# Attention, projection and routing of a decoder layer as one program, with P made transposed by a second score product

## What is computed

```python
x = x + mixer(layernorm(x), ...)
# attention, Q from layernorm(x), K and V from the context (8, 256, 256)
q = Q @ WQ + bQ;  k = K @ WK + bK;  v = V @ WV + bV          # split into 16 heads of 16
scores = einsum('bhqd,bhkd->bhqk', q, k) / 4
scores = where(causal, scores, -inf)
probs = softmax(scores, axis=-1)
x = x + einsum('bhqk,bhkd->bhqd', probs, v).reshape(B, L, 256) @ WO + bO
# experts, on layernorm(x): y is its input
logits = y @ router_w.T                                      # 2048 tokens, 8 experts
k_probs, k_idx = top_k(softmax(logits), 2);  k_probs = k_probs / sum(k_probs)
# rank of each pair within its expert by order of tokens, kept below a capacity of 641
h = silu(buf[e] @ w1[e]);  out_buf[e] = h @ w2[e]
x = x + y + sum over the 2 experts of k_probs * out_buf[expert, slot]
```

## Time and profile before

| | |
|---|---|
| median of 3 runs | 873.04 us (870.11 to 873.97) |
| the profiled execution | 866.73 us |
| its span, first to last instruction | 864.9 us |
| PE, PEld busy | 684.1 us (79%), 597.3 us (69%) |
| DVE, ACT, POOL busy | 599.8 us (69%), 434.1 us (50%), 349.4 us (40%) |
| granted TensorE clock, mean | 0.894 |
| DMA | 70.35 MB, mean 81 GB/s |

### The profile page before, as it was taken

The page is one execution under the profiler, slowest core; times in us unless marked ns, Lnnn a source line. Parts: engine busy times, 40 slices in busy tenths (PEclk is TensorE's granted clock), DMA queues, the critical chain, the costliest instruction groups (busy, mean ns, idle before and its releaser), DMA issues. The chain is left out here.

```text
span 864.9 us, 15113 instructions
## 1 busy us (share of the span) xinstructions
PE 684.1 (79%) x4776; PEld 597.3 (69%) x4792; DVE 599.8 (69%) x1285; ACT 434.1 (50%) x971; POOL 349.4 (40%) x322
## 2 busy tenths in 40 slices
PE   3759979889752199888988666509999999999992
PEld 2538768777542066666666556508999999999992
DVE  6685786867841089999999686704877877877831
ACT  4555736535411077777777311104655655655641
POOL 1357352343403000000000437752477777777755
PEclk9898999999975599999999765557999999999997
DMA  9102018230211611111111423223055255251213
GB/s 299 29 26 88 24 50 291 71 117 20 88 49 49 204 37 49 47 45 44 49 48 26 140 80 104 78 67 132 5 143 148 30 145 147 30 146 18 27 22 41
DMA packets 54857, 70.35 MB, mean 81 GB/s; under 512 B 10843, under 2 KB 45542, under 8 KB 54800
## 3 DMA queue, kind: packets, MB, share of 16 engines
q1 hardware_dynamic: 45584, 61.82, 22.1%
q0 software_dynamic: 9216, 7.81, 6.3%
HBM read 42.57 MB, written 28.79 MB: 83 GB/s over the span
## 5 line engine op out<-in xcount | busy, mean ns | idle before, releaser
L1114 ACT ACTIVATE a_pr<-a_scores,a_nm 128x128 f32<-128x128 f32 (+1 forms) x256 | 90.6, 426 | 80.8 <-DVE a_nm L1186 77.6
L1694 DVE SCALAR_TENSOR_TENSOR w_v<-w_th,w_bank 128x324 f32<-128x324 f32 x128 | 62.9, 492 | 70.6 <-ACT w_th L1424 69.3
L1563 PE MATMUL w_bank<-w_w2h,w_hh 128*108 128x256 f32 x384 | 108.6, 283 | 0.5 <-POOL w_hl L1349 0.5
L1563 PE MATMUL w_bank<-w_w2h,w_hl 128*108 128x256 f32 x384 | 107.8, 281 | 0.0
L1563 PE MATMUL w_bank<-w_w2l,w_hh 128*108 128x256 f32 x384 | 107.5, 280 | 0.0
L1424 ACT ACTIVATE w_th<-w_bank 128x324 f32<-128x324 f32 x128 | 56.6, 442 | 100.0 <-PE w_bank L102 99.9
L1349 POOL TENSOR_TENSOR w_hl<-w_v,w_hh 128x324 fp32r<-128x324 f32 x64 | 56.4, 882 | 91.5 <-ACT w_hh L1430 91.5
L1183 DVE TENSOR_REDUCE a_mx<-a_scores 128x2 f32<-128x512 f32 (+1 forms) x96 | 65.4, 681 | 34.1 <-remote 33.5
L1365 POOL IOTA w_x<- 128x16 uint32 x1 | 0.2, 191 | 205.9 <-POOLq L1077 205.9
L102 PE MATMUL w_bank<-w_xh,w_w1h 128*128 128x324 f32 x256 | 81.1, 317 | 1.1 <-ACT w_xh L1419 1.1
L102 PE MATMUL w_bank<-w_xh,w_w1l 128*128 128x324 f32 x256 | 80.8, 316 | 0.0
(11 more groups left out here) (230 smaller groups left out, 1995.6 us busy)
## 6 DMA issues: line engine op xcount, KB each, us to landing
w_s<-in_L_ffn_w SPq DMA_DIRECT2D x16, 1024.0 KB, 5.9
disp<-c_blank SPq DMA_DIRECT2D x8, 658.1 KB
w_rows<-disp SPq DMA_DIRECT2D x8, 658.1 KB
vd<-m_vs SPq DMA_DIRECT2D x4, 816.0 KB, 3.7
a_vs<-vd SPq DMA_DIRECT2D x1, 3264.0 KB, 11.1
g_x<-in_x SPq DMA_DIRECT2D x4, 512.0 KB, 7.9
m_cin<-in_ctx SPq DMA_DIRECT2D x4, 512.0 KB, 4.3
kd<-m_qkh SPq DMA_DIRECT2D x4, 512.0 KB, 2.9
```

Source lines behind the costliest of these rows:

```text
L1114: ins = act.activation(pr[:, u % 2, j * n:(j + 1) * n], sbank[u % 3][:, j * n:(j + 1) * n], ACT.Exp, bias=nm[:, u, j:j + 1], scale=SCALE)
L1563: mm = pe.matmul(eb[t // 2][0:SP_, (t % 2) * D:(t % 2 + 1) * D], a[:, g % 3, s], w2_piece(b, f), start=f == 0 and t % 2 == 0 and n == 0, s ...
L1694: dve.scalar_tensor_tensor(v[:, n % 4, :], th[:, n % 2, :], 1.0, hb[n % 3][:, 0:HALF], ALU.add, ALU.mult).then_inc(F["v"], 1)
```

## The change

The mixer stays, but for V: DVE writes V with its bias once, in fp32, into `vf`, where each head has 32 columns, 16 of V and 16 of zeros (`VP`); the splitting on ACT and POOL goes, and `vd` is 2048 x 512 fp32. WO is no longer loaded or split there.

Attention, projection and routing become one block, `attention_route_experts`, of which one step serves a third of a batch and half. There are 16 groups g (8 batches b, 2 halves k of the heads) of 3 steps, so 48 steps. In a group there are 8 heads, as 4 pairs p and 2 row halves e (partitions 0 to 63 and 64 to 127). Rows 0 to 15, 16 to 31 and 32 to 47 of each half hold Q high, high, low and K high, low, high, so that one matmul with 48 rows makes the split product.

- Scores are made twice. Once as queries by keys, six steps ahead (LEAD), for the maxima alone: `mask(u)`, `scores(u)`, and one reduction of 1024 columns on DVE (`maxima(u)`). Then as keys by queries (`turned_mask`, `turned`), where K has two more rows of -1 and Q two more rows that hold the maxima, high and low, so that the product comes out with the maximum subtracted.
- To get there the maxima of a group are turned by PE (`turn_maxima`), split by ACT and DVE, and written into Q's rows by 16 DMAs of one row each (`maxima(g)` on SP).
- ACT takes one exponential of 1024 columns per step, from PSUM to SBUF in fp32. This is P transposed; no transpose and no split follows.
- The product with V has V stationary (32 columns) and P moving, in fp32, the four heads of a set in four groups of 32 output rows; the same again with ones gives the sums (`weigh`). DVE takes a reciprocal of 128 x 256 and multiplies (`divide`), which leaves the output transposed, as the projection needs it.
- Projection (fp32, WO not split) and routing of each block are spread over later steps: `batch_due` and `due` say that batch b is projected at step 8 + 6b, and that block i of 512 tokens has its layer norm at 12i + 16, its logits at 12i + 20, its ranks at 12i + 23, and its 8 scatters at steps 12i + 24 to 12i + 31. The layer norm's scaling moves from DVE to ACT.
- SP lays each group's Q and K by 12 DMAs of 64 KB (16 rows x 4 pairs x 256). Four groups have room (ITEMS); group g + 2 is laid ahead of the maxima of group g.
- The scores and the turned scores have one pair of PSUM banks each, so that a step of PE waits for DVE's reduction and ACT's exponential of the step before.

The diff, cut to its core:

```diff
-                def lay(b, k):
-                    ge(sp, S[f"s{k}"], UPC * b)
-                    for src, q, kx in ((0, qh, kxh), (1, ql, kxl)):
-                        sp.dma_start(q[:, k, :].bitcast(F32), qd[src][k * P:(k + 1) * P, bass.ds(b * L, L)]).then_inc(S[f"laid{k}"], 16)
-                        for h in range(HPC):
-                            rows = slice(h * HD, (h + 1) * HD)
-                            sp.dma_start(kx[rows, k, h, :].bitcast(F32), kd[src][k * P + h * HD:k * P + (h + 1) * HD, bass.ds(b * L, L)])\
-                                .then_inc(S[f"laid{k}"], 16)
...
+                def lay(g):
+                    b, k = divmod(g, 2)
+                    ge(sp, A["st"], 3 * (g - ITEMS + 1))
+                    for m, srcs in ((q3[g % ITEMS], (qd[0], qd[0], qd[1])), (k3[g % ITEMS], (kd[0], kd[1], kd[0]))):
+                        for n, src in enumerate(srcs):
+                            heads = src[k * P:(k + 1) * P, b * L:(b + 1) * L].rearrange("(p e r) t -> e r p t", p=4, e=2)
+                            for e in range(2):
+                                at = 64 * e + HD * n
+                                sp.dma_start(m[at:at + HD, :, :].bitcast(F32), heads[e]).then_inc(A[f"laid{g % ITEMS}"], 16)
+                def maxima(g):
+                    sp.wait_ge(A["ml"], g + 1)
+                    for n in range(2):
+                        for e in range(2):
+                            for p in range(4):
+                                at, h = 64 * e + 3 * HD + n, 4 * e + p
+                                sp.dma_start(q3[g % ITEMS][at:at + 1, p, :].bitcast(F32), mt[g % 2][h:h + 1, n, :].bitcast(F32))\
+                                    .then_inc(A[f"m_in{g % 2}"], 16)
...
+                for g in range(GR):
+                    if ITEMS <= g + 2 < GR:
+                        lay(g + 2)
+                    maxima(g)
+                    if g == 0:
+                        weights(1)
+                    if g % 2 == 1 and 3 <= g and (g - 3) // 2 + 2 < B:
+                        values((g - 3) // 2 + 2)
+                    if g % 4 == 3 and g >= 7:
+                        store_base((g - 7) // 4)
...
+                def exps(n):
+                    act.wait_ge(A["st"], n + 1)
+                    ge(act, A["pv"], n - 2)
+                    act.activation(pr[n % 3][:, :], tbank[:, :], ACT.Exp, scale=SCALE).then_inc(A["exp"], 1)
...
+                                lhs = ones[:, h, :] if part else v32[b % 2][:, t, head * VP:(head + 1) * VP]
+                                mm = pe.matmul(obank[g % 2][32 * j:32 * j + 32, part * L + L - w:part * L + L], lhs,
+                                               pr[n % 3][:, at:at + w], start=s == 0 and part == 0, stop=True,
+                                               skip_group_check=True)
...
+                for t in range(-LEAD, END):
+                    u = t + LEAD
+                    if batch_due(t) is not None:
+                        project(batch_due(t))
+                    for j in range(2):
+                        if due(t, TURN + j) is not None:
+                            x3_turn(due(t, TURN + j), j)
+                    if due(t, LOGITS) is not None:
+                        logits(due(t, LOGITS))
+                    if due(t, RANKS) is not None:
+                        ranks(due(t, RANKS))
+                    if 0 <= t < NS:
+                        turned_mask(t)
+                    if u < NS:
+                        mask(u)
+                    if 0 <= t < NS:
+                        turned(t)
+                    if u < NS:
+                        scores(u)
+                    if t % 3 == 0 and 0 <= t // 3 + 1 < GR:
+                        turn_maxima(t // 3 + 1)
+                    if 1 <= t <= NS:
+                        weigh(t - 1)
...
+                    if u < NS:
+                        maxima(u)
+                    if t % 3 == 0 and 0 <= t // 3 + 1 < GR:
+                        maxima_low(t // 3 + 1)
+                    if t % 3 == 0 and 1 <= t // 3 <= GR:
+                        divide(t // 3 - 1)
```

More of the change, by code:

```diff
@@ L37 @@
 NEG = -1e30
-VW = HD + 1
-VT = HEADS * 3 * VW
+VP = 2 * HD
 MIX = {}
@@ L314, in _ @@
                 sp.wait_ge(S["k_st"], 32 * NBLK)
-                for n in range(2):
-                    sp.wait_ge(S[f"v_st{n}"], 16 * NBLK // 2)
+                sp.wait_ge(S["v_st"], 16 * NBLK)
                 sp.wait_ge(S["blanked"], 16 * E)
@@ new lines, in mask @@
+                def mask(u):
+                    s = u % 3
+                    ge(pe, A["nm"], u)
+                    for e in range(2):
+                        bank = sbank[:, e * 4 * P:(e + 1) * 4 * P]
+                        out = bank.rearrange("q (p k) -> q p k", p=4) if s == 0 else \
+                            bank.rearrange("q (p k) -> q p k", p=2)[:, :, P:2 * P]
+                        n = 4 if s == 0 else 2
+                        pe.matmul(out, c["identb"][:, :], c["mask"][:, :].unsqueeze(1).to_broadcast([P, n, P]),
+                                  start=True, stop=False, skip_group_check=True)
@@ new lines, in scores @@
+                def scores(u):
+                    g, s = divmod(u, 3)
+                    if s == 0:
+                        pe.wait_ge(A[f"laid{g % ITEMS}"], LAID * (g // ITEMS + 1))
+                    q, kx = q3[g % ITEMS], k3[g % ITEMS]
+                    todo = [(p, e) for p in (range(4) if s == 0 else (2 * s - 2, 2 * s - 1)) for e in range(2)]
+                    for n, (p, e) in enumerate(todo):
+                        rows, keys = slice(64 * e, 64 * e + 3 * HD), P if s == 0 else L
+                        tok = slice(0, P) if s == 0 else slice(P, L)
+                        at = e * 4 * P + (p if s == 0 else p % 2) * keys
+                        mm = pe.matmul(sbank[:, at:at + keys], q[rows, p, tok], kx[rows, p, 0:keys], start=False,
+                                       stop=True, skip_group_check=True)
+                    mm.then_inc(A["s"], 1)
@@ new lines, in turned_mask @@
+                def turned_mask(n):
+                    s = n % 3
+                    ge(pe, A["exp"], n)
+                    for e in range(2):
+                        bank = tbank[:, e * 4 * P:(e + 1) * 4 * P]
+                        out = bank.rearrange("k (p q) -> k p q", p=4) if s == 2 else \
+                            bank.rearrange("k (p q) -> k p q", p=2)[:, :, 0:P]
+                        m = 4 if s == 2 else 2
+                        pe.matmul(out, c["mask"][:, :], c["identb"][:, :].unsqueeze(1).to_broadcast([P, m, P]),
+                                  start=True, stop=False, skip_group_check=True)
@@ new lines, in project @@
+                def project(b):
+                    if b == 0:
+                        pe.wait_ge(S["rw"], 16 * 9)
+                    pe.wait_ge(A["o"], 2 * b + 2)
+                    if b % 2 == 0:
+                        ge(pe, S["xt"], b)
+                    else:
+                        pe.wait_ge(S["x2"], b)
+                    for t in range(2):
+                        for k in range(DC):
+                            at = (b % 2) * L + t * P
+                            mm = pe.matmul(bank0[:, t * D:(t + 1) * D], ot[:, k, at:at + P], wo[:, k, :],
+                                           start=k == 0, stop=k == DC - 1)
+                    mm.then_inc(S["y"], 1)
```

600 lines of the change are left out of this document (253 added, 347 removed).

## The result

| | before | after |
|---|---|---|
| median | 871.58 us (867.26 to 873.97, 4 runs) | 904.91 us (904.56 to 905.85, 4 runs) |
| profiled execution, span | 866.73, 864.9 us | 904.72, 903.0 us |
| granted TensorE clock, mean | 0.894 | 0.858 |

The change is slower: a ratio of 1.039, 95% interval 1.0345 to 1.0435. The prediction was 860 us, range 838 to 896, with 0.34 on slower: wrong in sign and outside the range.

What follows compares the result with a forecast made beforehand. SP's queue of DMA issues was to bound the groups at 13.5 us each; with start, last steps and tail the fetch came 11.7 us earlier, 12.7 with the mixer, giving 854.0 profiled, plus 6.3: 860 us, range 838 to 896.

Steps and rivals of the forecast that it cites:

- The step that failed: In SP's queue, every DMA issue was priced at about 0.473 us whatever its size, the sixteen maxima rows included.
- its 61 issues: SP's issues ahead of the first maxima, put at 28.9 us, plus 2 us for one stall.
- SP's queue: Main forecast for the groups: 28 issues at 0.473 us, 13.5 us per group with other transfers; chance 0.52.
- the cheap side: Rival on SP's issues: 0.42 us each, 12.6 us per turn of the maxima, 844 us in all; chance 0.15.
- The loop: From one group's maxima to the next: landing 2.0 us, chain of engines 3.9, sixteen issues 7.6, together 13.5 us.
- PE as the bound: Rival: matmuls in `weigh` take turns and tiling changes cost; at 16 us per group about 901 us, slower; chance 0.20.
- The clock: Rival: PE idles at landings and gets a lower clock; 15 us per group, 881 us, no gain; chance 0.13.
- The tail: Last block's chain from V's product through projection and routing to the scatters' landing: 33.2 us, after three steps of about 3 us.

Runs made afterwards that it cites:

- the kernel by way of DRAM: The changed kernel with each group's maxima written to DRAM by one DMA and brought back by two, instead of 16 one-row DMAs: 821.65 us, ratio 0.9464.
- the kernel whose waits are gone: The kernel by way of DRAM with the transposes of a normed block one step later (TURN 18 instead of 17): 806.39 us, ratio 0.9312.
- the kernel with four kinds: The changed kernel without its row DMAs, plus 16 transfers per group into an unread array, in four forms by turns: 865.8 us (before: 865.37).

## Why the prediction was wrong

**The step that failed.** "An issue costs SP this whatever it moves: 16 KB or 128 KB." The rows that stood for it differ in size and share their kind, DRAM to on-chip memory. The sixteen new issues are of another kind, on-chip to on-chip and cut in 32 packets, and cost SP 0.63 us each. Their term, 16 x 0.473 = 7.6 us per group, measured 10.2 in the mean of the twelve groups (10.0 in most). The twelve loads came out at 6.7 instead of 5.7, mostly by one issue of about 1.4 us among them (457.22 above). That issue is not the rows' doing: in the kernel by way of DRAM the loads still take 6.2 in the mean, 5.5 (2.66 + 2.77) without such an issue and up to 6.8 with one. What makes it long stays open.

Term by term, from the sum as predicted to the trace: SP's start and its 61 issues 1.9 us early; the first two groups' maxima, up to 335.0, 2.3 late in total; twelve groups with loads 206.5 us instead of 162 (17.2 each, not 13.5), which is 44.5 of the 49.9 us; the last two 28.8 instead of 27; landing 1.2 instead of 2.0; steps and tail 44.3 instead of 42.2. Of the 3.7 us per group the rows are 2.6, the loads 1.0 and the load of V and the store 0.1.

**Where the forecast was right.** SP's queue bounds, without a hole, PE waits for `a_q<-a_mt` at each group, DVE is at 43% ("under 60"). The text named as its failure "an issue of one row costs other than 0.47", but beside a doubt of 0.05 either way it worked out only the cheap side, 0.42, taken from a row of the same kind. An operation that no row showed had to be bounded from both sides, and this one was not.

**The loop.** I had it equal to the queue: 2.0 + 3.9 + 7.6 = 13.5. Measured it is 4.5 us from the last row's issue to the next group's first (540.95 to 545.43) plus 10.1, 14.6 us. The 4.5 stand where I had 2.0 + 3.9: PE starts 1.1 us after the last issue's end (542.06), and the rest is 3.4, since the chain goes there from PE's transposes of the maxima (to 544.57) straight to the two copies, without the reduction that I had put in. The rows made both longer; the queue, 17.2, is the longer one, as it also carries the loads, which no longer fit into the wait.

**PE as the bound.** The rival said slower, and slower it was, but not by this; the sign came true by another mechanism. V's product in PE's timeline after, in mid-stage:

```profile
441.44 0.64 PE L1411 MATMUL a_out<-a_pr,a_v 128*32 128x256 f32 x8
441.89 0.61 PE L1411 MATMUL a_out<-a_pr,a_ones 128*32 128x256 f32 x8
442.44 0.23 PE L1473 MATMUL a_shared<-w_both,c_onesb 128*128 128x24 bf16 x3
```

Four fp32 products of 256 columns (recorded as eight) start to start in 0.45 us. Four of the same length on all 128 columns of the array, the projection, take 1.99 at the same granted clock of 1.00, and 1.83 to the start of the next matmul (427.91):

```profile
426.08 1.99 PE L1439 MATMUL a_shared<-w_wo,a_ot 128*128 128x256 f32 x8
```

So the four column groups do run side by side: 4.1 times as fast from start to start. By FP8 and Floating Point Precision (TensorE Precision Notes) of the Trainium skill true FP32 takes four passes; 1024 columns at 0.45 ns would then be 1.84 us alone and 0.46 side by side, and the traces agree with both. The 5.5 us that I took as the least for V's product per group is 2.7 at the full clock (four sets of 256 columns at 0.45 and four of 128 at 0.22, 579.88 to 580.12). Three steps of PE in the midst of waiting took about 10.2 us (436.41 to 446.6), in the range of 10 to 12, and PE is the fullest engine once the rows are cheap, at 11.0 to 12.5 us per group, which gains and doesn't lose. What the changes between matmuls of full, half and quarter size cost was not isolated.

**The clock.** 0.78 in the groups against 0.98 in attention before. PE waited for 82 us there, as that rival said, but the clock is not the cause: the sixteen rows take SP 10.0 to 10.8 us in all twelve groups, and the clock is back at 0.96 in the kernel whose waits are gone. There it came as a second gain beside the 8.1 us of waiting.

**The tail.** It is right within 2.1 us of 42.2, with errors of both signs. The last product with V is done 9.4 us after the landing, where 9.0 and 2.0 had been put; the division, with the wait for it, took 3.8 instead of 1.1, since a reciprocal alone takes 1.76; the projection 3.44 at the lower clock, instead of 3.0. In the mixer 2.4 us went, not 1 (Q's store is issued at 266.29 instead of 268.69); the kernels here differ among themselves by up to 3.8 us at SP's first load after the mixer (276.63 to 280.38), so that is within what this part varies.

## What to carry to other kernels

A price read from rows holds for the kind in the rows: before a DMA's issue price is multiplied by hundreds, compare source and destination memory and the number of packets, not only size, and where no row matches, say what twice the price would do to the sum. If many small transfers stand in a loop in which an engine waits for them, count the issues first: here three issues through DRAM, with one more landing, beat sixteen direct ones by 81 us. The Trainium skill's advice on many small transfers (DMA: Bandwidth & Descriptors, Rules for kernel authors) is to coalesce them; the 25 us between sixteen and two issues from DRAM bear that out. The kind of issue was worth twice as much here, 55 us.

## What the hardware showed that I had not expected

- An issue on SP from on-chip to on-chip memory took 0.63 us (in the kernel with four kinds 0.63 to 0.71), for 1 KB as for 16 KB; on-chip to DRAM 0.28 to 0.33 for 16 KB; one DRAM row of 1 KB to one on-chip row 0.29; DRAM to 16 rows, 64 KB, 0.46 (2.77 for six). The first issue of a load behind such a row transfer took 0.58 (454.25 above), the others around it 0.43.
- An on-chip row of 1 KB to one on-chip row moved as 32 packets, 16 of 64 bytes and 16 of 4; the same row out of DRAM as 2.
- A reciprocal on DVE costs four times the multiplication of the same size out of the same bank (groups of instructions after, 309 to 571 us: busy us, mean ns):

```profile
L1583 DVE RECIPROCAL a_rc<-a_out 128x256 f32<-128x256 f32 x14 | 24.6, 1758 | 12.9 <-PE a_out L1411 12.9
...
L1586 DVE TENSOR_TENSOR a_ot<-a_out,a_rc 128x256 f32<-128x256 f32 x14 | 5.9, 424 | 0.5
```

- VectorE: DVE Perf Modes (First, the fixed hardware budget) of the Trainium skill says that the reciprocal is an iterative divide with a repeat count of 8; 1758 against 424 ns agrees in kind, at a factor of 4.1.
